# Value tiles in every second turn of the late batches, and the loads and low halves of experts 1, 2 and 6 to 8 put further ahead

## The chip, the cores and the metric

The kernel runs on one core of a Trainium2 chip. The metric is the time of one execution on the device in microseconds (us), the median of several runs. The core has a matrix engine (TensorE, PE in the profile), three engines for element-wise work (VectorE or DVE, ScalarE or ACT, GpSimd or POOL) and SyncE (SP), which here only issues DMAs.

## What is computed

One transformer block over 16 sequences of 256 rows with 512 features:

```python
x = x + xattn(layernorm(x), ctx)     # 16 query heads, 8 key/value heads, head size 128
h = layernorm(x)
x = x + moe(h) + (silu(h @ shared_gate) * (h @ shared_up)) @ shared_down
# moe: 32 experts of 512 x 256, each row picks 4 (2 of 4 groups, then top 4), capacity 128 rows per expert,
#      given out in order of the rows
```

The arithmetic is float32. The kernel writes every float32 operand as a float16 high half plus a float16 low half, and every product as three float16 matmuls (high by high, high by low, low by high).

## The kernel before, in words

**Attention.** The attention is cut into 128 turns, `i = 8 b + j`: batch b (a sequence), turn j (a key/value head with its two query heads). In turn i the matrix engine does, in this order: the scores of turn i, half of the query projection of turn i+1, a "first" filler into bank `ps_fill[1]`, the attended values of turn i-1 (`attend`), the other half of the query projection, a "second" filler into bank `ps_fill[0]`, the key projection of turn i+1 (again in `ps_fill[1]`), and the output projection of turn i-1 (`project`). Each step waits on semaphores for what the other engines have prepared. Scores go through DVE (`maxima`), ACT (`exps`), DVE (`prob_scales`), POOL (`probs_high`) and DVE (`probs_low`), are transposed by a DMA that SP issues (`turn_probs`), and come back as operand of `attend` in the next turn. Every engine has its own written-out order of the work of a turn; all of them call the same two tables, `first(b, j)` and `second(b, j)`, which say which filler the turn has.

**Fillers.** In batch b, with z = b - 1 and a = b + 1, the fillers are: four value tiles (`value`, six matmuls of 512 columns each) that make the value operand of batch a; the gate and the rank step of the router for batch z; and, for z < DEFER = 8, the shared feed-forward of batch z (four "up" and two "down" steps). A value tile costs work on ACT too (`value_high`, L896) and on DVE (`value_low`, L1215). For z >= 8 the shared feed-forward is put off to the end of the kernel, so that batches 9 to 14 have only the four value tiles, gate and rank: the tiles stand in turn 0 (second), turn 1 (first and second) and turn 2 (second). Batch 15 has no next batch, so it has no value tile at all.

**The norm of a finished batch.** The residual row block of batch z is finished in turn 0 and at the start of turn 1 of the next batch (`residual`, DVE L1180). Then follow, in turn 1: its statistics (DVE `x1_stats_row`, L1152 and L1157), the inverse deviation (POOL `inv_std`, L672 and L675), this turn's `probs_high` on POOL (L716 to L722), and behind it the normalisation (POOL `x1_norm`, L694, two instructions). ACT makes the high halves of it (`xn2_high`, L912) behind everything else of turn 1 and ahead of the `exps` (L980) of turn 2; DVE makes the low halves (`xn2_rest`, L1225) in turn 2 behind `maxima` and ahead of `prob_scales`. `project` waits for `head_low` (DVE L1317); the scores of the next turn wait for `query_low` (L1209) and `key_low` (L1204), which stand behind `probs_low` (L1312) on DVE.

**The tail.** After turn 127 the put-off shared feed-forward of eight batches is done in 48 pieces; 24 of them (k = 0 to 23) stand before the loop over the 32 experts and the others beside experts 0 to 23. Among the early pieces stands the routing of the last batch: `choose_*` and `find_slots` on DVE, `record` (eight indirect DMAs to a slot table, POOL L771), the load of the table (L838), the first gathers of rows (`gather`, L779), and `expert_rows(0)` on PE (L1823), which waits for gather 0. An expert has three weight parts of 512 KB (`part` 0 to 2). SP loads them into six float32 buffers (`load_expert`, L560 to L570; the load of expert e waits until the low half of the same part of expert e - 6 is made), ACT makes the high halves (`expert_high`, L1005) and DVE the low halves (`expert_low`, L1432) in three float16 buffers (HELD = 3). A piece k on DVE is two instructions (L1245, L1248), and for some k DVE also makes the low half of the result (`piece_rest`, L1257); for others POOL does both halves (`late_split`, L744 and L746). On PE piece k waits for piece k - 2 to be read (k < 24).

The schedule of the fillers:

```python
for i in range(TURNS + 1):        # PE; the other engines have loops of the same form
    filler(first(b, j), ps_fill[1]); attend(i - 1); query(i + 1, 1)
    filler(second(b, j), ps_fill[0]); key(i + 1); project(i - 1)
```

Of the kernel before, what the change touches and what calls it, by code (L numbers as in the profile page):

```python
# [14 lines left out]
B, T, D = 16, 256, 512  # L15
# [3 lines left out]
E, TOPK, GROUPS, TOPG = 32, 4, 4, 2  # L19
# [6 lines left out]
TB, SB, KD, KC, FB, FSB = T // P, S // P, D // P, DC // P, F // P, FS // P  # L26
# [23 lines left out]
AHEAD = 6  # L50
HELD = 3
# [4 lines left out]
DEFER = 8  # L56
# [42 lines left out]
def build(nc, x, ctx_t, mask, mask_cols, wq, wk, wv, wo, gate_t, gate_bias, w1, w2, w3,  # L99
          shared_gate, shared_up, shared_down, out):  # L100
    stack = ExitStack()
    with stack:
# [279 lines left out]
        def first(b, j):  # L382
            a, z = b + 1, b - 1
            if b == 0:
                return None
            if j == 1:
                return ("value", a, 0, 1) if a < B else None
            if j == 7:
                return ("down", z, 0) if z < DEFER else None
            return {3: ("gate", z), 6: ("rank", z)}.get(j)  # L390

        def second(b, j):
            a, z = b + 1, b - 1
            if b == 0:
                tiles = [(b_, half, s) for b_ in (0, 1) for half in range(2) for s in range(SB)]
                return ("value", *tiles[j]) if j >= SB else None
            if j < 3:
                return ("value", a, *((0, 0), (1, 0), (1, 1))[j]) if a < B else None
            if z >= DEFER:
                return None  # L400
            return ("up", z, j - 3) if j < 7 else ("down", z, 1)

        before = {}
        for bank_no, first_use in ((0, [("value", 0, 0, 1)]), (1, [("key", 0), ("value", 0, 0, 0)])):
            held = list(first_use)
            for i in range(TURNS):
                b, j = divmod(i, KV)
                filler = (second, first)[bank_no](b, j)
                if filler:
                    held.append(filler)  # L410
                if bank_no == 1 and i + 1 < TURNS:
                    held.append(("key", i + 1))
            before |= {b_: a_ for a_, b_ in zip(held, held[1:])}
            before["end", bank_no] = held[-1]
# [54 lines left out]
        def sync_program(sp):  # L469
# [70 lines left out]
            def load_x2t(n):  # L540
                sp.wait_ge(out_x2t, 16 * KEPT)
                sp.wait_ge(pe_up, ups(n - 4, FSB))
                sp.dma_start(x2t_place[n % 4].rearrange("p h k t -> p (h k t)"), x2t_kept[n - 4]).then_inc(
                    in_x2t[n - 4], 16)
# [15 lines left out]
            def load_expert(e, part):  # L560
                if e >= E:
                    return
                if e < AHEAD:
                    sp.wait_ge(pe_query, TURNS)
                    if over_wo(e):
                        sp.wait_ge(pe_out, TURNS)
                else:
                    sp.wait_ge(expert_lo[part], e - AHEAD + 1)
                sp.dma_start(expert_in[e % AHEAD][:, part * THIRD:(part + 1) * THIRD], (w1, w3, w2)[part][e].rearrange(
                    "(p k) n -> p (k n)", p=P)).then_inc(in_expert[part][e % AHEAD], 16)  # L570
# [20 lines left out]
            for i in range(TURNS):  # L591
                b, j = divmod(i, KV)
# [29 lines left out]
            load_x2t(4)  # L622


            for e in range(AHEAD - 2, E):
                for part in range(3):
                    if e + 2 - part >= AHEAD:
                        load_expert(e + 2 - part, part)
                if AHEAD <= e < AHEAD - 1 + KEPT:
                    load_x2t(e - AHEAD + 5)  # L630
# [243 lines left out]
        def act_program(act):  # L874
# [183 lines left out]
            for i in range(TURNS + 1):  # L1058
# [8 lines left out]
                if i < TURNS:  # L1067
                    filler(first(b, j), ps_fill[1])
                else:
                    piece(1)  # L1070
# [11 lines left out]
                if i < TURNS:  # L1082
                    filler(second(b, j), ps_fill[0])
# [59 lines left out]
        def dve_program(dve):  # L1143
# [93 lines left out]
            def piece(k):  # L1237
                kind, n, f = PIECES[k]
                if kind == "d":
                    return  # L1240
                u, ps = ups(n, f), piece_bank(k)
                dve.wait_ge(tanhed, u + 1)
                if k >= EARLY:
                    dve.wait_ge(ehid, k - EARLY + 1)
                dve.scalar_tensor_tensor(gated[:, :], tanh_g[:, :], 1.0, ps[:, 0:T], ALU.add, ALU.mult).then_inc(*own.up())  # L1245
                dve.wait_ge(*own.now())
                dve.wait_ge(glu_lo, u - 1 if k else u)
                dve.scalar_tensor_tensor(late_hidden[f % 2][:, :], gated[:, :], 0.5 * GLU * GLU * HS_S, ps[:, T:2 * T],  # L1248
                                         ALU.mult, ALU.mult).then_inc(hid, 1)

            def piece_rest(k):
                kind, n, f = PIECES[k]
                if kind == "d":
                    return
                both = late_h_t[n % 2]
                dve.wait_ge(glu_hi, ups(n, f) + 1)
                dve.scalar_tensor_tensor(both.lo[:, f, :], late_hidden[f % 2][:, :], 1.0, both.hi[:, f, :], ALU.mult,  # L1257
                                         ALU.subtract).then_inc(glu_lo, 1)
# [170 lines left out]
            def expert_low(e, part):  # L1429
                dve.wait_ge(expert_hi[part], e + 1)  # L1430
                at = slice(part * THIRD, (part + 1) * THIRD)
                dve.scalar_tensor_tensor(expert_w[e % HELD].lo[:, at], expert_in[e % AHEAD][:, at], W_S,  # L1432
                                         expert_w[e % HELD].hi[:, at], ALU.mult, ALU.subtract).then_inc(
                    expert_lo[part], 1)
# [58 lines left out]
            for i in range(TURNS + 1):  # L1493
                b, j = divmod(i, KV)
                z, a = b - 1, b + 1
# [30 lines left out]
                if live:  # L1526
                    prob_scales(i)
                    filler(first(b, j), ps_fill[1])
                else:
                    piece(1)  # L1530
# [12 lines left out]
                if i + 1 < TURNS:  # L1543
                    query_low(i + 1)

                early_key = live and second(b, j) is not None and second(b, j)[0] == "value"
                if i + 1 < TURNS and early_key:
                    key_low(i + 1)
# [28 lines left out]
            z = B - 1  # L1577
# [29 lines left out]
            pick(position)  # L1607
            find_slots(z)
            piece_rest(10)
            for k, e, part in ((11, 0, 2), (14, 1, 0), (15, 1, 1), (16, 1, 2)):  # L1610
                piece(k)
                if k > 11:
                    expert_low(e, part)
                piece_rest(k)
                if k == 11:
                    expert_low(e, part)
            piece(17)
            for part in range(3):
                expert_low(2, part)
            piece(20)  # L1620
            dve.wait_ge(in_table, 16)
            dve.tensor_scalar(slot_weight[:, :], table[:, :, 1].bitcast(F32), 0.5 * GLU * GLU * HE_S / ROUTE_SCALE,
# [319 lines left out]

        block = stack.enter_context(nc.Block())
        block.sync(sync_program)
        block.gpsimd(pool_program)
        block.scalar(act_program)
        block.vector(dve_program)
        block.tensor(pe_program)

# [26 lines left out]
```

## Time and profile before

| | |
|---|---|
| median of 3 runs | 1642.79 us (1641.42 to 1643.33) |
| the profiled execution, its own time | 1645.73 us |
| span of its trace | 1644.0 us |
| PE busy | 1602.1 us, 97% |
| DVE busy | 1216.7 us, 74% |
| ACT busy | 827.0 us, 50% |
| POOL busy | 818.7 us, 50% |
| mean granted TensorE clock | 0.993 |

All times of the trace are counted from the start of the span. An engine is busy while it executes an instruction that works on data; waiting for semaphores and issuing DMAs is not counted. Ends of matmuls are modelled and overlap the next one, so starts are the more reliable reading: the distance from the first score matmul of one turn to that of the next is the length of the turn. Batches 1 to 8 take about 89.4 us each, batches 9 to 14 about 74 us; the attention ends at about 1330 us, and the expert loop starts at about 1398 us.

### The profile page before, as it was taken

To read this page: it belongs to the slowest core of one execution; us is meant where nothing else is said; L and a number is where in the kernel's file an instruction comes from. 1 tells how busy PE (TensorE), PEld (TensorE's weight loads), DVE (VectorE), ACT (ScalarE), POOL (GpSimd) and SP (SyncE) were. 2 spreads that over 40 slices of the span, in tenths; PEclk is the share of its full clock that TensorE was granted. 3 is DMA by queue.
4 is the path that set the end of the run, shared out by engine and by line. 5 is a ranking of instruction groups with operands and counts; after the bars stand their busy time and mean duration, and the time that the engine had idled before them with its cause. 6 is when DMAs were issued, how large, how long until landed. Compare 5 with 4: busy or idle time off the path is not lost. (4 is left out here: it accounts for less than half of the span.)

```text
span 1644.0 us, 34926 instructions
## 1 busy us (share of the span) xinstructions
PE 1602.1 (97%) x12194; PEld 1149.3 (70%) x12194; DVE 1216.7 (74%) x3510; ACT 827.0 (50%) x2050; POOL 818.7 (50%) x1130
## 2 busy tenths in 40 slices
PE   7999999999999999999999999999999999999994
PEld 4767777777777686777777777777777777666641
DVE  7987676767767676767677778787787766687883
ACT  5764443534344443444354454544454443777782
POOL 3444554536354645445455564646464456354453
PEclk9999999999999999999999999999999999999997
DMA  8754433434334333434354545545444476899984
GB/s 242 186 142 84 82 81 78 96 67 98 69 88 72 88 76 78 85 78 85 69 120 79 105 96 114 113 87 108 91 108 87 104 260 181 266 280 292 301 209 59
DMA packets 395053, 205.69 MB, mean 125 GB/s; under 512 B 347888, under 2 KB 356080, under 8 KB 394880
## 3 DMA queue, kind: packets, MB, share of 16 engines
q1 hardware_dynamic: 380720, 181.32, 44.8%
q0 software_dynamic: 13600, 21.10, 6.9%
q8 instruction: 99, 1.62, 0.4%
q10 hardware_dynamic: 560, 1.05, 0.2%
q14 instruction: 74, 0.61, 0.1%
HBM read 87.67 MB, written 32.41 MB: 73 GB/s over the span
## 5 line engine op out<-in xcount | busy, mean ns | idle before, releaser
L980 ACT ACTIVATE arena<-arena,neg_max 128x256 f32<-128x256 f32 x512 | 253.7, 496 | 379.5 <-DVE neg_max L1297 319.0
L716 POOL TENSOR_SCALAR arena<-arena,prob_scale 128x256 f16<-128x256 f32 x384 | 183.4, 492 | 454.0 <-DVE prob_scale L1306 452.2
L1656 PE MATMUL ps_query<-xn_both,arena 128*128 128x256 f16 x1024 | 279.8, 273 | 1.5 <-DMA xn_both<-xn_half 1.5
L1657 PE MATMUL ps_query<-xn_both,arena 128*128 128x256 f16 x1024 | 279.8, 273 | 0.0
L1658 PE MATMUL ps_query<-xn_both,arena 128*128 128x256 f16 x1024 | 279.8, 273 | 0.0
L1297 DVE CUSTOM_DVE_ANT_0 arena<-ps_score,mask_add 128x256 f32<-128x256 f32 x512 | 186.7, 420 | 120.6 <-PE ps_score L1658 119.7
L1312 DVE SCALAR_TENSOR_TENSOR arena<-arena,prob_scale 128x256 f16<-128x256 f32 x384 | 231.7, 651 | 7.6 <-POOL arena L716 7.6
L1656 PE MATMUL ps_out<-arena,o_t 128*128 128x512 f16 x512 | 194.1, 379 | 4.2 <-DVE o_t L1317 4.2
L1657 PE MATMUL ps_out<-arena,o_t 128*128 128x512 f16 x512 | 194.0, 379 | 0.0
L1658 PE MATMUL ps_out<-arena,o_t 128*128 128x512 f16 x512 | 194.0, 379 | 0.0
L771 POOL DMA_INDIRECT slot_table<-entry,slot_at x128 | 132.9, 1039 | 48.1 <-issue 33.6
L1317 DVE SCALAR_TENSOR_TENSOR o_t<-ps_head,o_t 128x512 f16<-128x512 f32 x128 | 88.4, 690 | 86.4 <-ACT o_t L993 85.6
L1656 PE MATMUL ps_score<-k_both,q_t 128*128 128x256 f16 x512 | 139.6, 273 | 2.3 <-DVE q_t L1209 1.6
L1656 PE MATMUL ps_head<-arena 128*128 128x256 f16 x512 | 139.5, 272 | 1.3 <-DMA arena<-arena 1.3
L1658 PE MATMUL ps_score<-k_both,q_t 128*128 128x256 f16 x512 | 139.6, 273 | 0.0
L1657 PE MATMUL ps_score<-k_both,q_t 128*128 128x256 f16 x512 | 139.5, 273 | 0.0
L1658 PE MATMUL ps_head<-arena 128*128 128x256 f16 x512 | 139.5, 272 | 0.0
L1657 PE MATMUL ps_head<-arena 128*128 128x256 f16 x512 | 139.5, 272 | 0.0
L993 ACT ACTIVATE o_t<-ps_head 128x512 f16<-128x512 f32 x128 | 76.0, 594 | 104.1 <-PE ps_head L1658 92.4
L1432 DVE SCALAR_TENSOR_TENSOR arena<-arena 128x1024 f16<-128x1024 f32 x96 | 116.7, 1230 | 0.0
L1656 PEld LDWEIGHTS ps_query<-xn_both,arena 128*128 128x128 f16 x1024 | 100.5, 98 | 13.8 <-DMA xn_both<-xn_half 1.8
L1657 PEld LDWEIGHTS ps_query<-xn_both,arena 128*128 128x128 f16 x1024 | 100.4, 98 | 11.9
(341 smaller groups left out, 4067.8 us busy)
## 6 DMA issues: line engine op xcount, KB each, us to landing
arena<-w SPq DMA_DIRECT2D x96, 512.0 KB, 6.7
x_in<-x SPq DMA_DIRECT2D x15, 512.0 KB, 4.1
xn_rows<-xn_half SPq DMA_DIRECT2D x15, 512.0 KB
out_rows_dram<-x SPq DMA_DIRECT2D x30, 256.0 KB
ctx_in<-ctx_t SPq DMA_DIRECT2D x16, 256.0 KB, 3.0
weight_in<-wq SPq DMA_DIRECT2D x8, 512.0 KB, 5.1
weight_in<-wo SPq DMA_DIRECT2D x8, 512.0 KB, 4.4
arena<-arena SPq DMA_TRANSPOSE x256
```

Source lines behind the costliest of these rows:

```text
L716: pool.tensor_scalar(p_rows[:, c, 0, :], probs[:, c, :], prob_scale[:, c:c + 1], 1.0, ALU.mult, ALU.mult).then_inc(norm_hi, 1)
L771: pool.indirect_dma_start(slot_table, bass.IndirectOffsetOnAxis(ap=slot_at[z % 2][:, t, k:k + 1], axis=0), entry[z % 2][:, t, k, :], None, ...
L980: act.activation(probs[:, c, :], probs[:, c, :], ACT.Exp, bias=neg_max[:, c:c + 1], scale=-1.0, accum_out=prob_sum[:, c:c + 1]).then_inc(e ...
L993: act.activation(o_t.hi, ps_head[:, :], ACT.Copy, scale=1.0 / P_S).then_inc(head_hi, 1)
L1297: dve.tensor_tensor_reduce(out=probs[:, c, :], in0=ps_score[h][:, t * S:(t + 1) * S], in1=mask_add[b % 2][:, :], scale=-SCORE_SCALE, scala ...
L1312: dve.scalar_tensor_tensor(p_rows[:, c, 1, :], probs[:, c, :], prob_scale[:, c:c + 1], p_rows[:, c, 0, :], ALU.mult, ALU.subtract).then_in ...
L1317: dve.scalar_tensor_tensor(o_t.lo, ps_head[:, :], 1.0 / P_S, o_t.hi, ALU.mult, ALU.subtract).then_inc(head_lo, 1)
L1432: dve.scalar_tensor_tensor(expert_w[e % HELD].lo[:, at], expert_in[e % AHEAD][:, at], W_S, expert_w[e % HELD].hi[:, at], ALU.mult, ALU.sub ...
L1656: pe.matmul(dst, a.hi, b.hi, start=start and n == 0, stop=False)
L1657: pe.matmul(dst, a.hi, b.lo, start=False, stop=False)
L1658: m = pe.matmul(dst, a.lo, b.hi, start=False, stop=stop and n == len(pairs) - 1)
```

## The change

Four edits. In `first` and `second`: in batches 9 to 14 the four value tiles stand in turns 0, 2, 4 and 6, all as "second" fillers, where they stood in turns 0, 1, 1 and 2. Their order and number are the same. SP loads experts 6, 7 and 8 whole, in this order, ahead of the staggered loop; before, parts were staggered by expert (part 0 of expert 7 ahead of part 1 of expert 6, and so on). On DVE the low halves of expert 1 are made behind piece 11 (they were spread over pieces 14 to 16), those of expert 2 behind pieces 14, 15 and 16 (they came together behind piece 17). In pieces 14 to 16 the low half of the piece now stands ahead of that of the expert.

```diff
@@ def first(b, j) @@
-            if j == 1:
+            if j == 1 and z < DEFER:
                 return ("value", a, 0, 1) if a < B else None
@@ def second(b, j) @@
+            if z >= DEFER:
+                return ("value", a, *divmod(j // 2, SB)) if a < B and j % 2 == 0 else None
             if j < 3:
                 return ("value", a, *((0, 0), (1, 0), (1, 1))[j]) if a < B else None
-            if z >= DEFER:
-                return None
             return ("up", z, j - 3) if j < 7 else ("down", z, 1)
@@ sync_program @@
-            for e in range(AHEAD - 2, E):
+            for e in range(AHEAD, AHEAD + HELD):
                 for part in range(3):
-                    if e + 2 - part >= AHEAD:
+                    load_expert(e, part)
+            for e in range(AHEAD, E):
+                for part in range(3):
+                    if e + 2 - part >= AHEAD + HELD:
                         load_expert(e + 2 - part, part)
                 if AHEAD <= e < AHEAD - 1 + KEPT:
                     load_x2t(e - AHEAD + 5)
@@ dve_program @@
-            for k, e, part in ((11, 0, 2), (14, 1, 0), (15, 1, 1), (16, 1, 2)):
+            for k, lows in ((11, ((0, 2), (1, 0), (1, 1), (1, 2))), (14, ((2, 0),)), (15, ((2, 1),)), (16, ((2, 2),))):
                 piece(k)
-                if k > 11:
-                    expert_low(e, part)
                 piece_rest(k)
-                if k == 11:
+                for e, part in lows:
                     expert_low(e, part)
             piece(17)
-            for part in range(3):
-                expert_low(2, part)
             piece(20)
```

## Rows read from the trace of the kernel before

**Rows 1.** The page, busy time, share of the span and instructions of PE.
```profile
PE 1602.1 (97%) x12194; PEld 1149.3 (70%) x12194; DVE 1216.7 (74%) x3510; ACT 827.0 (50%) x2050; POOL 818.7 (50%) x1130
```
**Rows 2.** Waits of PE in batches 9 to 14: releaser, total us, times, longest.
```profile
PE ps_head L1656 <- DMA arena<-arena: 0.7, 3, 0.3
PE ps_out L1656 <- DVE o_t L1317: 0.3, 1, 0.3
```
**Rows 3.** PE timeline, batch 12: first score matmuls of turns 1 to 5.
```profile
1045.22 0.27 PE L1656 MATMUL ps_score<-k_both,q_t 128*128 128x256 f16 x1
...
1056.30 0.27 PE L1656 MATMUL ps_score<-k_both,q_t 128*128 128x256 f16 x1
...
1066.08 0.27 PE L1656 MATMUL ps_score<-k_both,q_t 128*128 128x256 f16 x1
...
1075.16 0.27 PE L1656 MATMUL ps_score<-k_both,q_t 128*128 128x256 f16 x1
...
1083.65 0.27 PE L1656 MATMUL ps_score<-k_both,q_t 128*128 128x256 f16 x1
```
**Rows 4.** PE timeline, batch 15: score starts of turns 1 to 3, one `project`.
```profile
1267.65 0.27 PE L1656 MATMUL ps_score<-k_both,q_t 128*128 128x256 f16 x1
...
1276.61 0.27 PE L1656 MATMUL ps_score<-k_both,q_t 128*128 128x256 f16 x1 [0.32 <-issue]
...
1284.19 0.39 PE L1656 MATMUL ps_out<-arena,o_t 128*128 128x512 f16 x1 [1.52 <-DVE o_t L1317]
...
1286.79 0.27 PE L1656 MATMUL ps_score<-k_both,q_t 128*128 128x256 f16 x1
```
**Rows 5.** POOL timeline, batch 15, turn 1.
```profile
1273.21 1.56 POOL L716 TENSOR_SCALAR arena<-arena,prob_scale 128x256 f16<-128x256 f32 x3
...
1276.10 4.13 POOL L694 TENSOR_SCALAR weight_in<-x,mean_var,rstd 128x512 f32<-128x512 f32 x2
```
**Rows 6.** ACT timeline, batch 15, turn 2: its first exponential.
```profile
1280.80 0.49 ACT L980 ACTIVATE arena<-arena,neg_max 128x256 f32<-128x256 f32 x1
```
**Rows 7.** DVE timeline, batch 15, turns 1 and 2.
```profile
1267.85 1.29 DVE L1180 SCALAR_TENSOR_TENSOR x<-ps_out,x_in 128x512 f32<-128x512 f32 x2 [0.33 <-PE ps_out L1658]
...
1273.73 1.85 DVE L1312 SCALAR_TENSOR_TENSOR arena<-arena,prob_scale 128x256 f16<-128x256 f32 x3 [0.38 <-POOL arena L716]
...
1276.10 0.41 DVE L1204 SCALAR_TENSOR_TENSOR k_both<-ps_fill,k_both 128x256 f16<-128x256 f32 x1
...
1283.44 0.69 DVE L1317 SCALAR_TENSOR_TENSOR o_t<-ps_head,o_t 128x512 f16<-128x512 f32 x1 [0.17 <-ACT o_t L993]
```
**Rows 8.** PE, DVE and POOL timelines, batch 13, turn 1.
```profile
1119.52 0.27 PE L1656 MATMUL ps_score<-k_both,q_t 128*128 128x256 f16 x1
...
1119.97 1.27 DVE L1180 SCALAR_TENSOR_TENSOR x<-ps_out,x_in 128x512 f32<-128x512 f32 x2
...
1125.32 1.56 POOL L716 TENSOR_SCALAR arena<-arena,prob_scale 128x256 f16<-128x256 f32 x3
...
1128.16 4.31 POOL L694 TENSOR_SCALAR weight_in<-x,mean_var,rstd 128x512 f32<-128x512 f32 x2
```
**Rows 9.** Waits of PE from 1320 to 1570 us: releaser, total us, times, longest.
```profile
PE ps_head L1656 <- DMA arena<-arena: 0.6, 2, 0.3
...
```
**Rows 10.** DVE timeline, pieces 14 and 17 and the low halves of expert 2.
```profile
1373.57 0.42 DVE L1245 SCALAR_TENSOR_TENSOR gated<-tanh_g,ps_fill 128x256 f32<-128x256 f32 x1 [3.85 <-issue]
...
1382.52 0.41 DVE L1245 SCALAR_TENSOR_TENSOR gated<-tanh_g,ps_query 128x256 f32<-128x256 f32 x1
...
1383.30 4.16 DVE L1432 SCALAR_TENSOR_TENSOR arena<-arena 128x1024 f16<-128x1024 f32 x3
```
**Rows 11.** POOL timeline, low half of piece 17 and gather 0.
```profile
1384.87 1.52 POOL L746 TENSOR_TENSOR ctx_both<-mask_add,ctx_both 128x256 f16<-128x256 f32 x1
...
1386.56 1.97 POOL L779 DMA_INDIRECT x_in<-xn_rows,table  x1 [0.17 <-issue]
```
**Rows 12.** PE timeline, first transposition of gathered rows (`expert_rows(0)`).
```profile
1394.24 0.28 PE L1823 MATMUL ps_fill<-blank,x_in 128*128 128x128 f16 x2
```

## The prediction

> **What bounds the kernel now.** I read the page first: PE is busy for 97% of the span [rows 1]. So what counts is PE's own waits in the stretches that the change touches. In batches 9 to 14 they are 1.0 us together [rows 2]; from 1320 to 1570 us, which holds all the pieces and low halves that are moved, 0.6 us is the only wait of note [rows 9]. (A row of waits understates each gap by up to 0.16 us, since the modelled end of a 256-column matmul, 0.27 us after its start, overlaps the next one.) The change takes no matmul away. A filler is worth its place only where it covers a wait, and the first question is what the tiles that leave turns 1 and 2 were covering.
>
> **Turn lengths.** From the first score matmul of a turn to that of the next, in batch 12 [rows 3]: turn 1 with two tiles 1056.30 - 1045.22 = 11.08 us, turn 2 with one tile 9.78, turn 3 with the gate 9.08, turn 4 with nothing 8.49. A tile is thus 1.29 us of PE, and turn 1 is exactly a bare turn and two tiles (8.49 + 2 x 1.29 = 11.07): no wait in it. Moving a tile between turns with no wait costs nothing.
>
> **Batch 15 is a sample of what is left.** It has no tiles. Its turn 1 takes 1276.61 - 1267.65 = 8.96 us and its turn 2 takes 10.18 us [rows 4]: 0.47 and 1.69 us over a bare turn. The chain, read over the engines: the residual and statistics sit ahead of and in turn 1 on DVE (from 1267.85 [rows 7]); POOL makes the inverse deviation behind them and begins `probs_high` only at 1273.21, 5.56 us into the turn [rows 5]; DVE waits for it, begins `probs_low` at 1273.73 and ends the key at 1276.51 [rows 7], and PE's next scores follow 0.10 us later [rows 4]. That is the 0.47. Behind `probs_high` POOL normalises, from 1276.10 to 1280.23 [rows 5]; ACT must make high halves of the result ahead of its exponentials, which begin at 1280.80, 4.19 us into turn 2 [rows 6]; `head_low` ends at 1284.13 [rows 7], and `project` stood idle for it [rows 4]. That is the 1.69. In batches 9 to 14 the two tiles of turn 1 hide all this: the chain counts from the start of turn 1, and 2.58 us of other PE work pass beside it.
>
> **The change, part by part.**
>
> Turn 0 keeps its one tile: no change.
>
> Turn 1 loses both tiles and becomes batch 15's turn 1: 0.47 us over bare. One thing differs. With a tile in turn 0, its low half on DVE stands ahead of the residual, and in batch 13 everything is later: residual 0.45 us into the turn instead of 0.20, `probs_high` 5.80 instead of 5.56 [rows 4, 5, 7, 8]. Nothing in the chain has slack (DVE waits for POOL, PE for DVE), so I add 0.24: 0.71 us, turn 1 at 9.20 us.
>
> Turn 2 keeps one tile. On PE it stands ahead of `project`, so it covers 1.29 of batch 15's 1.69: 0.40 us is left, turn 2 at 10.18 us. Both the start of turn 2 and the end of the normalisation move by the same 0.24, so the difference stays. The tile's ACT work delays `key_high`, its DVE work stands behind `key_low`; `query_low` is the later one there, so neither decides. The bounds of this term: 0 if the normalisation ends earlier, 1.69 if the tile covers nothing; I take 0.40, as its terms are direct rows.
>
> The normalisation took 4.31 us in batch 13 and 4.13 in batch 15 [rows 5, 8]; I take 4.13, as in batch 15 turn 1 has no tile either. With 4.31 it would be 0.18 x 6 = 1.1 us more. The Trainium skill (SBUF — State Buffer, section "SBUF: two separate sides") says that GpSimd and a DVE instruction with two SBUF inputs exclude each other for a whole instruction; by it the longer time comes from DVE's last `probs_low` next to the start of the normalisation, which fits either row.
>
> Turns 4 and 6 gain a tile each: 9.78 us and turn 6 likewise 1.29 more. ACT gains 0.7 and DVE 0.7 us of work there beside 1.29 more of PE, so they fall no further behind; no cost.
>
> DVE now makes `head_low` of turn 1 ahead of `probs_low` instead of behind its first two; batch 15 does the same, so it is in the 0.47.
>
> Sum per batch: 0.71 + 0.40 = 1.11 us, in six batches 6.7 us.
>
> SP: the order of the loads of experts 6 to 8. No engine waits for an expert load anywhere in the tail by the waits, so an earlier load gives nothing to PE. The loads behind keep their conditions. What SP now has ahead of the second kept operand load is the low half of expert 2 part 2, which is made earlier than before. Cost zero; its cover is that lead of several us.
>
> DVE: behind piece 11 three more low halves. One is 1.39 us at most (4.16 / 3 [rows 10]) and 1.2 us alone; DVE stood idle for 3.85 us ahead of piece 14 [rows 10], so 3.7 us fit by a hair, up to 0.3 us late if not. Behind piece 16 a low half comes after `piece_rest` instead of before it; piece 17, which began at 1382.52 [rows 10], begins about 0.6 us later, and PE's piece 19 may wait 0.2 us. Behind piece 17 4.16 us of DVE fall away [rows 10], where DVE then idles. Tail in all: +0.2, between -0.6 (the wait of rows 9) and +1.5.
>
> Transposes that come late from the DMA: `attend` of turn 1 now comes 1.29 us earlier, without the first filler. A late transpose was waited for at most 0.3 us in one place [rows 2]; it could now be 0.3 + 1.29 = 1.6 us. Up to 0.7 us of that is absorbed by the wait at the end of the same turn. I put +0.1 in the sum.
>
> Total 6.7 + 0.2 + 0.1 = 7.0 us. The trace's span would go from 1644.0 to 1651.0; the profiled execution took 1645.73 us, 2.9 us over the median of 1642.79, so on the median I forecast 1649.8 us.
>
> **The rivals.**
>
> A, no stall, same time: with a tile in turn 0, as in the other batches, the engines enter turn 1 rested, and batch 15's waits belong to batch 15 alone (its turn 0 had none). For it: batch 15's turn 0 is itself slower than bare. Against it: every step of the chain in batch 13 is as late or later, counted from the start of turn 1 [rows 5, 8]. It gives 1642.8 us; the existing waits [rows 2, 9] could bring it down to 1641. This is the side "not slower". It decides if `probs_high` of turn 1 starts under 5.1 us into the turn.
>
> B, the transposes: the loads of the next x block and of the mask run beside the second transpose of turn 0's probabilities, and without the first filler PE's `attend` in turn 1 waits for that transpose in most of the six batches. For: the tiles covered 1.29 us of it, and the rows show only the remainder. Against: batch 15 shows no such wait (but loads no x either). Price: about 0.6 to 1.0 us past what the turn's end absorbs, in six batches 4 to 6 us more, 1654.8 us.
>
> C, the router's tail: four low halves in a row stand beside POOL's `record` DMAs, and the loads of experts 6 to 8 beside the scatter and the table; gather 0 (issued at 1386.56 [rows 11]) comes later and PE's `expert_rows(0)` at 1394.24 [rows 12] waits. Price 1 to 3 us, 1652 us. Against it: what held gather 0 back was POOL's split of piece 17, 1.52 us for its second instruction beside DVE's low halves [rows 11], and that neighbour is gone. The same page and section of the Trainium skill name just this (two SBUF inputs on DVE against GpSimd reading SBUF); by it gather 0 is rather 1 us earlier.
>
> D, a gain: DVE and SP free the tail and PE gains. Only 0.6 us is there to gain [rows 9], so it cannot pass 0.2%.
>
> **How the numbers follow.** About 0.2% (3.3 us) is what a measurement of this kernel can tell from no change. Forecast 0.60; A 0.18, B 0.12, C 0.07, D 0.03 (D and a part of A bring the time down, by more than 0.2% or not). The predicted time is the forecast's, 1649.8. Its own bounds: turn 1 alone (0.47 x 6 = 2.8 us, 1645.6) to both terms with the longer normalisation and 1.5 us of tail (1652.5). The range 1645.5 to 1654.5 holds the forecast, C, and the lower part of B, and leaves out A. Slower: forecast, B, C = 0.79, less a little for a forecast that lands under 3.3 us: 0.77. Same: 0.18. Faster: 0.05.
>
> **What would show it.** In the trace after: turns 1 of batches 9 to 14 at 9.2 us, turns 2 at 10.2, turns 4 and 6 at 9.8 and 9.9, each batch about 1.1 us longer than before; PE's waits in this stretch at 4 to 6 us, most of them `project` for `head_low` and scores for DVE; batches 1 to 8 and 15 unchanged; the expert loop starting as much later as the attention ended. It is wrong if turn 1 is 8.5 us long (A), if the wait is named as a DMA (B), or if `expert_rows(0)` has a wait ahead of it (C).

## The result and the profile after

The changed kernel takes 1652.32 us (median of 8 runs, 1646.64 to 1656.14) against 1642.79 us (8 runs, 1641.42 to 1648.58) for the kernel before on the same chip: ratio 1.0059, 95% interval 1.0048 to 1.0070, so 7.9 to 11.5 us slower. The profiled execution took 1652.68 us with a span of 1651.0 us, against 1645.73 and 1644.0 before. The forecast was 1649.8 us on the median and 1651.0 for the span.

The page: the same instructions, 97% of a longer span.

```profile
span 1651.0 us, 34926 instructions
...
PE 1604.6 (97%) x12194; PEld 1148.5 (70%) x12194; DVE 1218.5 (74%) x3510; ACT 827.7 (50%) x2050; POOL 819.1 (50%) x1130
```

Where the 7.0 us of span are, by the first score matmuls: batch 9 begins 0.6 us later (813.7 after 813.1; the start of the kernel varies, see below), batches 9 to 14 take 452.6 us after 445.6, and from the start of batch 15 to the first expert product it is 138.5 us after 139.1. So the stretch with the moved tiles carries 7.0 us and the tail no loss. The waits of PE in batches 9 to 14, for those of [rows 2]:

```profile
PE ps_head L1656 <- DMA arena<-arena: 2.6, 5, 1.0
PE ps_score L1656 <- issue: 1.5, 5, 0.3
PE ps_out L1656 <- DVE o_t L1321: 1.1, 5, 0.2
```

Two of the three are as foretold: the next scores (five times, for DVE, whose instruction shows as "issue") and `project` for `head_low`. The first, `attend` waiting for a transposition, is half of the 5.2 us, where I had expected next to nothing. PE timeline of batch 11, first score matmuls of turns 1, 2 and 3, for [rows 3]:

```profile
974.14 0.27 PE L1656 MATMUL ps_score<-k_both,q_t 128*128 128x256 f16 x1
...
983.10 0.27 PE L1656 MATMUL ps_score<-k_both,q_t 128*128 128x256 f16 x1 [0.31 <-issue]
...
993.28 0.27 PE L1656 MATMUL ps_score<-k_both,q_t 128*128 128x256 f16 x1
```

Turn 1 is 8.96 us long and turn 2 10.18 us. All six batches have 8.95 to 8.96 in turn 1, and five have 10.18 in turn 2 (batch 12: 10.70). Turns 4 and 6 are 9.78 and 9.90 us long, a tile more than 8.49 and 8.61, but for batch 13, which has 10.24 and 10.61. The chain of the norm in the same turns, on DVE, POOL and ACT, for [rows 5 to 8]:

```profile
974.35 1.29 DVE L1184 SCALAR_TENSOR_TENSOR x<-ps_out,x_in 128x512 f32<-128x512 f32 x2 [0.70 <-PE ps_out L1658]
```
```profile
979.71 1.56 POOL L720 TENSOR_SCALAR arena<-arena,prob_scale 128x256 f16<-128x256 f32 x3
...
982.59 4.13 POOL L698 TENSOR_SCALAR weight_in<-x,mean_var,rstd 128x512 f32<-128x512 f32 x2
```
```profile
987.29 0.49 ACT L984 ACTIVATE arena<-arena,neg_max 128x256 f32<-128x256 f32 x1
```

`probs_high` begins 979.71 - 974.14 = 5.57 us into turn 1, not 5.80 [rows 8]; the normalisation takes 4.13 us; ACT's exponentials begin 987.29 - 983.10 = 4.19 us into turn 2. It is batch 15 of the kernel before, to a hundredth [rows 4 to 6].

### The profile page after: what moved, and what is told of

Its sections match the earlier page's. It is cut to its first block and busy times, and to the rows that moved or that the text cites. A ratio compares the mean times of both kernels' runs of the same rounds, so it can differ in the third digit from the quotient of the medians.

```text
span 1651.0 us, 34926 instructions
## 1 busy us (share of the span) xinstructions
PE 1604.6 (97%) x12194; PEld 1148.5 (70%) x12194; DVE 1218.5 (74%) x3510; ACT 827.7 (50%) x2050; POOL 819.1 (50%) x1130
```

## The experiments

Nine kernels ran, in three groups; the kernels of a group shared a chip and the runs of the kernel before. Executions differ: in the eleven traces (before, after and the nine) the first scores come between 18.4 and 21.8 us, and the medians of the kernel before in the first two groups were 1646.16 (34 runs) and 1644.79 us (17 runs). So differences under some 3 us are read from turn lengths, not from totals.

**Is it the tiles or the tail?** One kernel with the two edits of `first` and `second` alone, one with the loads and low halves alone (the tile tables as before). Their edits are the first two and the last two hunks of the change:

```diff
-            if j == 1:
+            if j == 1 and z < DEFER:
...
+            if z >= DEFER:
+                return ("value", a, *divmod(j // 2, SB)) if a < B and j % 2 == 0 else None
```
```diff
+            for e in range(AHEAD, AHEAD + HELD):
...
+            for k, lows in ((11, ((0, 2), (1, 0), (1, 1), (1, 2))), (14, ((2, 0),)), (15, ((2, 1),)), (16, ((2, 2),))):
```

> Only the move of the value tiles; loads and low halves as before. My theory (the tiles of turns 1 and 2 covered the chain of the norm): this part is the whole loss, turn 1 of batches 9 to 14 at 8.96 us, turn 2 at 10.18 us, the time 7 to 10 us over the kernel before, like the changed kernel. Rival (the tail carries a part of the loss): clearly less than the changed kernel's 9.5 us, 5 us or less.

> Only the tail's part (experts 6 to 8 loaded whole, low halves of experts 1 and 2 ahead); tiles as before. Theory: PE had 0.9 us of gaps there between 1364 and 1381 us, so 0 to 1 us faster than before, within the noise. Rival (late loads or gathers): 1 to 3 us slower, with a wait ahead of the first transposition of gathered rows. It also shows whether in turn 0 of batches 10 to 15 ACT's copy of the attended values again starts 1.6 us after PE's last matmul of them, as in the trace before; with the tiles in the old places I expect that it does.

Tiles alone: 1651.54 us (11 runs), ratio 1.0030 (1.0016 to 1.0043) to its kernel before, 2.6 to 7.1 us slower. Turn 1 is 8.97 us in all six batches, turn 2 10.18 or 10.19 in five (11.00 in batch 12). The whole span is 1651.1 us, as with both parts. By its ratio the loss is 4.9 us, below the 7 to 10 us that I had expected and within what I had given to the rival (5 us or less); what decides against the rival is the tail alone. Tail alone: 1644.40 us (12 runs), ratio 0.9992 (0.9977 to 1.0006): no difference that can be measured, and 11.07, 9.78 us for turns 1 and 2 as before. Its waits of PE from 1320 to 1570 us are 0.5 us for 0.6 before [rows 9]:

```profile
PE ps_head L1655 <- DMA arena<-arena: 0.5, 2, 0.3
```

So the tiles are the loss. The ratio of the tiles alone is milder than the first measurement (1.0030 for 1.0059) and the intervals do not touch. The turn lengths are the same in both traces; why the medians differ stays open. My side expectation on ACT was wrong: its copy of the attended values in turn 0 is not late here although the tiles stand in the old places.

**How much cover do turns 1 and 2 need?** One kernel with one tile in each of turns 0, 1, 2 and 4, one with none in turns 0 to 2. The edits, in `second` for one tile a turn and for none in turns 0 to 2 (both have the changed `first`, and the tail of the kernel before):

```diff
+            if z >= DEFER:
+                return ("value", a, *divmod((0, 1, 2, 4).index(j), SB)) if a < B and j in (0, 1, 2, 4) else None
```
```diff
+            if z >= DEFER:
+                return ("value", a, *divmod(j - 3, SB)) if a < B and 3 <= j < 7 else None
```

> Tiles of batches 9 to 14 in turns 0, 1, 2 and 4, one in each; the tail as before. Theory: one tile (1.29 us) in turn 1 covers its 0.47 us and leaves the norm 0.8 us more before turn 2, so turn 1 is 9.78 us and turn 2 9.78 us, no loss: 1642 to 1644 us, equal to before. Rival (any thinning of turns 1 and 2 costs, or tiles in turns 4 and 6 cost): 3 us or more over before.

> Tail as before; the four tiles of batches 9 to 14 in turns 3 to 6. Theory: batches 9 to 14 become batch 15 in their first turns: turn 0 between 8.5 and 9.0 us, turn 1 8.96, turn 2 10.18 us, although it has a tile less than in the changed kernel; 0 to 0.5 + 0.47 + 1.69 us of waits a batch, 13 to 16 us over before. If turn 2 is 8.89 us (10.18 less a tile), a tile there costs its full 1.29 us and covers nothing, and my reading of turn 2 is wrong.

One tile a turn: 1647.17 us (12 runs), ratio 1.0002 (0.9988 to 1.0017). The scores of turns 1, 2 and 3 of batch 13:

```profile
1121.32 0.27 PE L1656 MATMUL ps_score<-k_both,q_t 128*128 128x256 f16 x1
...
1131.10 0.27 PE L1656 MATMUL ps_score<-k_both,q_t 128*128 128x256 f16 x1
...
1140.88 0.27 PE L1656 MATMUL ps_score<-k_both,q_t 128*128 128x256 f16 x1
```

9.78 and 9.78 us, with no wait: one tile in turn 1 covers what two covered, and a tile in turn 4 costs its own 1.29 us of PE and nothing else. No tiles in turns 0 to 2: 1659.26 us (4 runs), ratio 1.0093 (1.0072 to 1.0114), 11.8 to 18.8 us slower. The scores of turns 0 to 3 of batch 13, then the waits of PE in batches 9 to 14:

```profile
1119.93 0.27 PE L1657 MATMUL ps_score<-k_both,q_t 128*128 128x256 f16 x1
...
1128.41 0.27 PE L1657 MATMUL ps_score<-k_both,q_t 128*128 128x256 f16 x1
...
1137.38 0.27 PE L1657 MATMUL ps_score<-k_both,q_t 128*128 128x256 f16 x1 [0.32 <-issue]
...
1147.57 0.27 PE L1657 MATMUL ps_score<-k_both,q_t 128*128 128x256 f16 x1
```
```profile
PE ps_out L1657 <- DVE o_t L1318: 9.0, 6, 1.5
PE ps_score L1657 <- issue: 1.3, 4, 0.3
PE ps_head L1657 <- DMA arena<-arena: 0.2, 1, 0.2
```

8.48, 8.97 and 10.19 us (turn 1 is 8.73 in batch 10 and 9.13 in batch 11, turn 2 is 10.19 or 10.20 in all six). Turn 2 is as long with no tile as with one in the changed kernel: its length is set by the norm as long as the tiles in it stay under 1.69 us, and one tile is 1.29 us. Six waits of 1.5 us for `head_low` are the new part. Turn 0 needs no cover (8.48 to 8.75 us).

**Is it POOL's normalisation?** The changed kernel with the normalisation of batches 8 to 14 on DVE, behind `key_low` at the end of turn 1, and the same with the old tiles (the first hunk is POOL's program, the second DVE's):

```diff
-                if j == 1 and b:
+                if j == 1 and 0 < b <= DEFER:
                     x1_norm(z)
...
+                if j == 1 and routed and b > DEFER:
+                    x1_norm(z)
```

> The changed kernel, with the normalisation of batches 8 to 14 (in batches 9 to 15) made by DVE behind key_low at the end of turn 1 instead of by POOL. Theory: the normalised rows are there about 2.5 us earlier, ACT's exponentials of turn 2 start 1.5 us into the turn instead of 4.2; turn 2 falls from 10.18 to 9.78 us in batches 9 to 14 and from 10.18 to about 8.6 in batch 15, turn 1 stays at 8.96: 3 to 4 us less than the changed kernel. If turn 2 stays at 10.18 us, POOL's normalisation is not what holds it.

> Tiles as before, the tail as in the change, and the normalisation of batches 8 to 14 on DVE. Theory: in batches 9 to 14 the tiles cover everything anyway (turns 11.07 and 9.78 us as before); only batch 15's turn 2 falls from 10.18 to 8.48 us, and with the tail's 0 to 1 us this gives 1.5 to 2.5 us under the kernel before, the fastest of all. If the norm on DVE costs anything by itself, turn 1 of batches 9 to 14 grows over 11.07 us.

On the changed kernel: 1650.14 us (12 runs), ratio 1.0023 (1.0011 to 1.0036) to before; 1.4 us under the tiles alone, in the same group. The scores of turns 1 to 3 of batch 13, and of turns 2 and 3 of batch 15:

```profile
1124.42 0.27 PE L1658 MATMUL ps_score<-k_both,q_t 128*128 128x256 f16 x1
...
1133.39 0.27 PE L1658 MATMUL ps_score<-k_both,q_t 128*128 128x256 f16 x1 [0.32 <-issue]
...
1143.16 0.27 PE L1658 MATMUL ps_score<-k_both,q_t 128*128 128x256 f16 x1
...
1282.24 0.27 PE L1658 MATMUL ps_score<-k_both,q_t 128*128 128x256 f16 x1 [0.32 <-issue]
...
1290.72 0.27 PE L1658 MATMUL ps_score<-k_both,q_t 128*128 128x256 f16 x1
```

Turn 1 stays at 8.97, turn 2 falls to 9.77 us, and batch 15's turn 2 from 10.18 to 8.48 us. The normalisation on POOL is what held turn 2, and it is not what holds turn 1. By the turns this is worth 6 x 0.40 + 1.70 = 4.1 us; less shows in the median, and the changed kernel itself was not in this group. With the old tiles and the changed tail: 1645.27 us (12 runs), ratio 1.0001 (0.9988 to 1.0013). I had expected 1.5 to 2.5 us under the kernel before. Batch 15's turn 2 fell only to 9.09 us in its trace, since `attend` waited 0.5 us for a transposition there. The 1.1 us by which the turn did fall, and the 0 to 1 us expected of the tail, are below what the runs resolve. No version beat the kernel before by a difference that can be measured.

**The waits for transpositions.** In the changed kernel PE's `attend` waited for a transposition five times, by the waits shown above. In batch 12, turn 2, the wait and what the DMA queues moved in the 4.6 us ahead of it:

```profile
1061.41 0.27 PE L1656 MATMUL ps_head<-arena 128*128 128x256 f16 x1 [0.63 <-DMA arena<-arena]
```
```profile
q1 hardware_dynamic: 1864, 0.47, 77.8%
q8 instruction: 1, 0.02, 1.2%
q14 instruction: 1, 0.01, 0.5%
```

The columns are packets, MB and the share of 16 engines. The one packet of q8, a queue of instructions, is 16 KB and occupied one of the 16 DMA engines for 0.88 us, from 2.0 us ahead of the `attend` on, while the transposition was in flight. From batch 9 up to turn 126 the eleven traces have 39 waits of `attend` of 0.3 us or more. 37 of them have such a packet 2.0 to 3.0 us ahead; the other two (0.35 and 0.30 us, both in turn 0 of batch 12) have one 0.9 and 1.1 us ahead. There is one such packet in about 16 us, so a packet in that place by chance would be rare. Every trace has 99 of them. Counted along PE's own instructions (25417 but for the two kernels below: 12194 weight loads, 12194 matmuls, 1029 others, nearly all waits), a packet comes every 256: in each trace packet k starts when PE has started 256 k + 182 to 188 instructions (the median; four in five lie between 164 and 237). No other engine has enough instructions for that. That was a correlation with the waits; two kernels tested it, by more waits, fulfilled already, ahead of PE's first work (128 in one, 64 in the other):

```diff
+            for _ in range(128):
+                pe.wait_ge(consts, 1)
             pe.wait_ge(consts, CONSTS)
```

> The changed kernel once more, with the others of this call and the kernel before: the loss by the turns is 6 x (0.47 + 0.40) = 5.2 us, less up to 1 us of the tail; the rest of the 9.5 us of the first measurement would be waits of attend for a late transposition, which differ between executions. So 4 to 8 us over before. In the trace each such wait should have a 16 KB packet of the queue of instructions 2 to 3.5 us ahead of it.

> The changed kernel with 128 waits that are already fulfilled, at the start of PE's program. The 16 KB packets of the instruction queue come about once in 256 PE instructions, so they should come half a distance (some 7 us) elsewhere in the turns. Theory: the lengths of turns 1 and 2 (8.96 and 10.18 us) stay as they are, but the waits of attend for a transposition, which stood in turn 2 of batch 12 and turn 3 of batch 14 in three traces of this arrangement of tiles, leave these turns and come up in others or nowhere. Rival (the transposes are late by other DMAs of the kernel at those places): the waits stay in turn 2 of batch 12 and turn 3 of batch 14.

> The same with 64 waits, a quarter of the distance. Theory: the packets come some 3.5 us elsewhere than in the changed kernel, and the waits of attend again stand in other turns than turn 2 of batch 12 and turn 3 of batch 14, each with such a packet 2 to 3.5 us ahead. Rival: they stay in place.

The traces show a smaller shift than I expected: two of these waits went into one instruction, so PE has 25481 and 25449 instructions, 64 and 32 more. That is a quarter and an eighth of the distance between packets (some 4 and 2 us), not a half and a quarter. In both kernels the packets keep their place in PE's count.

The changed kernel again: 1652.12 us (6 runs), ratio 1.0044 (1.0027 to 1.0062), 4.4 to 10.2 us slower, with waits in turn 2 of batch 12 (11.08 us long) and turn 3 of batch 14 (10.00 us) as in the traces of the changed kernel and of the tiles alone. With 128 waits more (one run, 1659.55 us; 1647.33 before), these turns are 10.18 and 9.09 us long, free of waits, and waits stand in others, the longest in turn 2 of batch 13 (11.35 us). The single run says nothing of the time: 4 us of it lie in batch 0 alone. The wait in batch 13, and the queues in the 2.4 us ahead of it:

```profile
1143.12 0.27 PE L1656 MATMUL ps_head<-arena 128*128 128x256 f16 x1 [1.07 <-DMA arena<-arena]
```
```profile
q1 hardware_dynamic: 500, 0.13, 113.9%
q8 instruction: 1, 0.02, 2.5%
```

With 64 more (one run, 1655.38 us), turn 3 of batch 14 has 0.26 us left of its 0.84, but turn 2 of batch 12 still has a wait (10.92 us), against what I expected: a packet still came 1.3 us into that turn (1.4 in the changed kernel), since packets scatter by more than 32 instructions around their place. The waits thus follow the packets, and where these fall is a matter of how many instructions PE has ahead. In both kernels turn 1 was not 8.96 us in every batch, as I had expected, but up to 9.20 us, and 9.88 in batch 9 with 128 more; the last section comes back to this.

What the change took away is the slack. In batch 14 SP issues the transpositions of turn 2's probabilities, in the kernel before and in the changed one:

```profile
1212.65 2.61 SPq L557 DMA_TRANSPOSE arena<-arena  x2
```
```profile
1218.15 2.61 SPq L558 DMA_TRANSPOSE arena<-arena  x2
```

Turn 3 begins at 1215.52 and 1219.67: 2.87 us later before, 1.52 us after. The same happens a turn earlier: the transpositions of turn 1 are issued 1.48 us ahead of turn 2, for 3.36 before. In turn 1 less other work of PE follows behind the probabilities; in turn 2 the norm now delays them. A packet of instructions comes near this transposition in both traces; only after the change does it delay `attend`, by 0.84 us. Behind turns 3 and 5 nothing changed (in batch 13 1.67 and 1.47 us ahead of the next turn, before and after), so waits in turns 4 and 6 are of a kind that the kernel before has too. The tail alone, with the old tiles, shows it in batches 9 to 14:

```profile
PE ps_head L1655 <- DMA arena<-arena: 2.1, 3, 1.3
```

## Why the prediction was right, point by point

The sign, the mechanism and the span were right. The sum was put together from partly wrong terms, and that it met the span to a tenth is luck: 1.4 us too much in turn 1 and 0.8 in the tail stood against 1.8 too little for the transpositions and 0.6 for the start.

- Turn 1, 0.47 us a batch: right, 8.96 us in all six batches, and that a tile covers it is shown by the kernel with one tile a turn (9.78 us, no wait). Which steps of the chain make the 0.47 is read from the trace; no kernel shortened them.
- The further 0.24 us of turn 1: wrong. The step was that "with a tile in turn 0, its low half on DVE stands ahead of the residual" and that this makes the turn later. I took it from batch 13 [rows 8], and that batch was not a plain sample: in its turn 0 ACT's copy of the attended values, which waits for PE alone, began 1.7 us after PE's last matmul of them (below), so all of DVE's work there was late. In the changed kernel, with the same tile in turn 0, the residual begins 0.21 us into turn 1, not 0.45. The next batch would not have shown it: in the trace before, batches 10 to 14 all begin it at 0.45 or 0.46. Batch 9 is the one that differs, with the same tile in turn 0 and the residual 0.20 us into turn 1:

```profile
822.86 0.27 PE L1656 MATMUL ps_score<-k_both,q_t 128*128 128x256 f16 x1
...
823.06 1.29 DVE L1180 SCALAR_TENSOR_TENSOR x<-ps_out,x_in 128x512 f32<-128x512 f32 x2 [1.04 <-PE ps_out L1658]
```

All six should have been read before 1.4 us went into the sum.

- Turn 2, 0.40 us a batch: right, 10.18 us; POOL's normalisation as its cause is shown by the kernel with that step on DVE, and that a tile there costs nothing by the kernel without one. The 4.13 us for the normalisation was right.
- Turns 0, 4 and 6 at no cost: right.
- The transpositions: mis-sized. "I put +0.1 in the sum" and measured 2.6 - 0.7 = 1.9 us in the trace. The sign of being wrong "if the wait is named as a DMA (B)" was thus half met: 2.6 of the 5.2 us of waits are. I looked at turn 1, where `attend` comes 1.29 us earlier; the waits stand in turns 2, 3, 4 and 6 instead. Those in turns 2 and 3 are the change's: 2.0 to 2.5 us by the lengths of these turns in the three traces with the changed tiles (after, tiles alone, changed again) and none in the three with the old ones (before, tail alone, old tiles with the norm on DVE). Those in turns 4 and 6 are of the old kind (above). By all waits of `attend` the old tiles have 0.7, 2.1 and 0.7 us, the changed ones 2.6, 3.0 and 2.2, so 1.9 is the difference of this pair of traces and 1.4 that of the means. Rival B had the right resource at the wrong turn, and the wrong other side: not the loads of x and mask but packets of program.
- The tail, +0.2: it is -0.6 in the trace and nothing in the runs. The -0.6 belongs to the trace before: from the scores of turn 127 to the first expert product it has 76.3 us, the changed kernel 75.2, and so have the three traces with the old tail and other tiles. Rival C cost nothing, since the first transposition of gathered rows has no wait ahead of it. As I wrote, POOL's split of piece 17 took less beside an idle DVE (0.67 us for its second instruction for 1.52 beside DVE's low halves [rows 11]). This agrees with what the Trainium skill (SBUF — State Buffer, "SBUF: two separate sides") says of GpSimd and a DVE instruction with two SBUF inputs. But "by it gather 0 is rather 1 us earlier" was wrong, and there rival C had the mechanism right: in all seven traces with the changed tail gather 0 is issued 67.1 to 67.9 us after the scores of turn 127, for 64.6 to 65.1 with the old tail, since the load of the table lands some 5 us later; SP's loads of expert parts and of `x2t_kept` run beside it (1.02 MB on q1 in that time, none beside the table before). In the trace after:

```profile
1397.50 1.19 POOL L783 DMA_INDIRECT x_in<-xn_rows,table  x1 [3.22 <-DMA table<-slot_table]
```

The loads as the reason are argued; no kernel moved them alone.

- By the turns: 6 x (0.47 + 0.40) = 5.2, transpositions 1.9, tail -0.6, start 0.6: 7.1 of the 7.0 us of span. Batches 9 to 14 are the best measure of the change itself: 445.6, 446.3 and 445.5 us in the three traces with the old tiles, 452.6, 452.9 and 451.8 with the changed ones, 6.6 us by the means. The measured median moved by 9.5 us, since the profiled execution before lay 2.9 us over its median and the one after only 0.4 us. By the ratios of the two later groups it moved 4.9 us (tiles alone) and 7.2 us. The upper bound of the terms was added up wrongly: 1649.8 + 1.1 + 1.3 is 1652.2, not 1652.5; nothing hung on it.

Rival A (no wait with a tile in turn 0) is out by the turn lengths.

## What to carry to other kernels

Work that fills an engine which is the bound costs the same in every place, so ask only what stands behind it: here two tiles hid a chain over four engines that counts from the start of the turn, and a stretch that lacks the filler (the last batch) shows the bare length of that chain before anything is changed. Thin out a turn only down to the cover that its chain needs; the turn with one tile was as good as that with two. When a term is read from one instance of a repeated pattern, compare all the others first: here a second and a third agreed with it, and only the one that differed showed the cause. And when a difference between two traces is put down to a change, look at a third and a fourth: of 1.9 us of waits, a kernel with the old order had 1.4 as well.

## What the runs showed of the hardware

**Program packets delay transposing DMAs.** The packets of PE's program (16 KB), 2.0 to 3.0 us ahead of a wait, took 0.9 to 1.6 us of one DMA engine, and a transposition of the probabilities then landed late: up to 1.6 us of wait (turn 6 of batch 14 with one tile a turn, 10.22 us for 8.61) in an otherwise full PE. That the transposition, spread over the engines, waits for the one with the packet fits this and is argued; the traces kept here do not tell the engine of a packet. The Trainium skill (DMA: Bandwidth & Descriptors, "Queues, rings and completion order") says that a DMA engine takes the queue rows in turn, a packet at a time; the waits fit this, but the order within one engine is not in the traces. That it is PE's program and not another engine's follows from the count, one packet in 256 instructions of PE in all eleven traces, and from the shift by PE's instructions alone; the traces do not name the owner.

**PE's signal can come late.** In the trace before, in turn 0 of batches 10, 11, 12, 13 and 14, ACT's copy began well after PE's last matmul of the attended values, as the matmul and the copy of batch 13 show, and the waits of ACT from 813 to 1272 us sum up:

```profile
1113.53 0.27 PE L1658 MATMUL ps_head<-arena 128*128 128x256 f16 x1
```
```profile
1115.47 0.60 ACT L993 ACTIVATE o_t<-ps_head 128x512 f16<-128x512 f32 x1 [2.23 <-remote]
```
```profile
ACT o_t L993 <- remote: 11.5, 5, 2.7
```

Eight of the eleven traces have no such row, among them the two of the changed kernel, the tiles alone and the tail alone; with 128 more waits, and likewise with 64, it is back:

```profile
ACT o_t L997 <- remote: 9.0, 4, 2.6
```

and there turn 1 is 9.14 to 9.20 us long in batches 10, 11, 13 and 14 with a late copy and 8.97 in batch 12 (9.11 to 9.20 and 8.96 with 64 more): the 0.24 us that I had added is what this costs where turn 1 has no tile. The residual begins 0.39 to 0.46 us into these turns, for 0.20, so turn 1 grows by what its chain starts later. The 9.88 us of batch 9 with 128 more are not explained; `probs_high` comes 0.9 us late there. What makes the signal late, and in which executions, stays open; no run tested it. Whether it has a part in the 9.5 us of the first measurement is not shown.
